# Keeping the intermediate activations in HBM as bf16, through casting transfers on GpSimd's queue

## The reference

```python
x = x + _layernorm(_L0_attn_ref(_layernorm(x), mask, weight, bias))
x = x + _layernorm(_L0_ffn_ref(_layernorm(x), W_up, gate_w, expert_bias, lora_A, lora_B))
# _L0_attn_ref: einsum('bsk,nk->bsn', data, masked weight) + bias
# _L0_ffn_ref:  x @ W_up.T + delta,  delta = one_hot(argmax(x @ gate_w.T)) picks B_e (A_e x)
```

## Time and profile before

| | us |
|---|---|
| median of 2 runs | 1734.52 (1693.67 and 1775.36) |
| profiled execution | 1690.93 |
| its span, slowest core (core 4) | 1689.4 |
| spans of the 8 cores | 1678.3 to 1689.4 |
| PE busy | 1115.7 (66%) |
| DVE, ACT, POOL busy | 571.7, 404.1, 82.5 |
| closing stage, last matmul to end | about 90 |

### The profile page before, as it was taken

How to read it: one execution, slowest core, us unless ns; L and a number is a source line. 1 busy time by engine, 2 the same in 40 slices (tenths; PEclk the granted TensorE clock), 3 DMA queues, 4 the chain that set the end, 5 groups by cost and what they waited for, 6 DMA issues and landing times.

```text
span 1689.4 us, 26743 instructions; the slowest of 8 cores (1678.3 to 1689.4 us)
## 1 busy us (share of the span) xinstructions
PE 1115.7 (66%) x9240; PEld 869.9 (51%) x9240; DVE 571.7 (34%) x861; ACT 404.1 (24%) x1185; POOL 82.5 (5%) x96
## 2 busy tenths in 40 slices
PE   0122219898988989889321221599999999999800
PEld 0011107676777767667210110377777777777600
DVE  1355445455555555552534334100000000000580
ACT  1224412222222222212323323222222222222200
POOL 1000000000000000000000000000000000000151
PEclk9999999999999999999655555699999999999955
DMA  8820224777667776762333383222442442442299
GB/s 192 289 100 1 50 87 133 184 175 196 163 166 199 171 200 161 174 154 69 119 131 134 117 197 123 78 51 51 76 76 51 76 76 51 76 76 51 79 330 339
DMA packets 40000, 220.47 MB, mean 131 GB/s; under 512 B 4850, under 2 KB 4866, under 8 KB 21442
## 3 DMA queue, kind: packets, MB, share of 16 engines
q0 software_dynamic: 11792, 84.46, 25.5%
q1 hardware_dynamic: 23330, 100.74, 17.9%
q10 hardware_dynamic: 4752, 33.56, 5.3%
HBM read 252.86 MB, written 33.55 MB: 170 GB/s over the span
## 4 chain that ended last, share of the span: by engine, by line
PE 48%; DMA 19%; DVE 16%; issue 8%; ACT 6%; DVEq 1%; ACTq 0%; POOLq 0%; SPq 0%; POOL 0%
PE pm L382 39%; DMA mring<-mw 14%; DVE psj_i L310 4%; PE pt L219 4%; DVE wmb L353 3%; DVE sums_h L263 2%; ACT xbst L278 2%; PE pm L219 2%; ACT mo L547 2%; PE pm L396 2%; ACT junk L533 2%; DMA fm<-xmid 1%; DMA mo<-x 1%; DMA y<-wmb 1%; DVE cmp L573 1%
## 5 line engine op out<-in xcount | busy, mean ns | idle before, releaser
L382 PE MATMUL pm<-wmb,fm 128*128 128x256 bf16 x8192 | 953.9, 275 | 38.8 <-DVE zfm L597 0.7
L382 PEld LDWEIGHTS pm<-wmb,fm 128*128 128x128 bf16 x8192 | 791.9, 99 | 178.4 <-issue 80.7
L402 ACT ACTIVATE mo<-pm 128x256 bf16<-128x256 f32 x256 | 98.3, 384 | 816.1 <-PE pm L389 437.2
L310 DVE TENSOR_REDUCE psj_i<-mring 128x32 int32<-128x1024 int32 x128 | 156.2, 1220 | 222.2 <-DMA mring<-mw 215.8
L219 PE MATMUL pt<-identb,xbst 128*128 128x128 bf16 x264 | 47.2, 289 | 184.9 <-ACT xbst L278 175.4
L188 DVE TENSOR_REDUCE st_d<-acc_s 128x1 f32<-128x16 f32 x8 | 1.4, 170 | 490.8 <-ACT junk L410 490.1
L353 DVE TENSOR_TENSOR wmb<-wmb,bmpj 128x4096 bf16<-128x4096 bf16 x32 | 141.6, 4425 | 11.4 <-DMA wmb<-bw 8.3
L219 PEld LDWEIGHTS pt<-identb,xbst 128*128 128x128 bf16 x264 | 22.7, 115 | 209.3 <-issue 209.2
L410 ACT ACTIVATE junk<-pm 128x256 bf16<-128x256 f32 x256 | 98.3, 384 | 23.8 <-ACT mo L402 0.4
L219 PE MATMUL pm<-identb,mo 128*128 128x128 bf16 x152 | 27.3, 289 | 51.4 <-ACT mo L547 46.1
L225 DVE COPY fm<-pt 128x512 bf16<-128x512 bf16 x72 | 30.6, 424 | 81.5 <-PE pt L219 81.1
(11 more groups left out here) (129 smaller groups left out, 495.9 us busy)
## 6 DMA issues: line engine op xcount, KB each, us to landing
mring<-mw SPq DMA_DIRECT2D x128, 512.0 KB, 5.3
wmb<-bw POOLq DMA_DIRECT2D x32, 1024.0 KB, 10.1
wmb<-bu POOLq DMA_DIRECT2D x32, 1024.0 KB, 7.8
mo<-x POOLq DMA_DIRECT2D x12, 1024.0 KB, 26.4
xst<-x SPq DMA_DIRECT2D x10, 1024.0 KB, 6.9
xmid<-xst ACTq DMA_DIRECT2D x10, 1024.0 KB, 3.9
fm<-xmid SPq DMA_DIRECT2D x8, 1024.0 KB, 11.6
y<-fm ACTq DMA_DIRECT2D x8, 1024.0 KB, 15.8
```

The lines of the kernel that those rows point to most:

```text
L310: return e.tensor_reduce(out=psj_i32[:, (j % 2) * 256 + pc * 32:(j % 2) * 256 + (pc + 1) * 32], in_=mring[idx % 2][:, :].rearrange("p (g w ...
L382: return e.matmul(bank[0:128, 0:NS], fm[:, k * 1024 + i * 128:k * 1024 + i * 128 + 128], wmb[j % 2][:, k * NS:(k + 1) * NS], start=(k == 0 ...
L402: return e.activation(out=mo[:, i * 4096 + j * NS:i * 4096 + (j + 1) * NS], in_=bank[0:128, 0:NS], func=AF.Identity, accum_out=acc_s[:, i ...
```

## The change

`xmid` becomes a bf16 tensor. A transfer between f32 and bf16 has to be issued by POOL, so the store of the middle moves from ACT's queue to POOL's, and the load of the closing stage from SP's queue to POOL's. The f32 slots in SBUF stay as they are. Both get semaphores of the `dP` group, which the first stage used: stores dP4 to dP7, loads dP0 to dP3, each taken again after two chunks. Nothing else is moved: in POOL's stream the 16 stores now stand before the casting loads of the second product (L626 on), and the loads of chunk i+1 in the closing stage stand behind POOL's own addition (L671, half 1) of chunk i.

```diff
-    d_xmid = nc.dram_tensor("xmid", [T, D], F32, kind="Internal").ap()
+    d_xmid = nc.dram_tensor("xmid", [T, D], BF16, kind="Internal").ap()
...
-                xm_tok[(i, h)] = E("scalar", lambda e, i=i, h=h, ap_slot=slots[h][0]: e.dma_start(
+                xm_tok[(i, h)] = E("gpsimd", lambda e, i=i, h=h, ap_slot=slots[h][0]: e.dma_start(
                     out=d_xmid[i * 128:(i + 1) * 128, h * HALF:(h + 1) * HALF], in_=ap_slot),
-                    waits=[trh[h]], inc=store_sem(), amt=16)
+                    waits=[trh[h]], inc="dP%d" % (4 + (2 * i + h) % 4), amt=16)
...
-                semn = slots[h][1] or p6_sems[(2 * i + h) % 4]
                 def fdx(e, i=i, h=h, ap_slot=ap_slot):
                     return e.dma_start(out=ap_slot,
                                       in_=d_xmid[i * 128:(i + 1) * 128, h * HALF:(h + 1) * HALF])
-                td[h] = E("sync", fdx, waits=xw[h] + [xm_tok[(i, h)]],
-                          inc=semn, amt=16)
+                td[h] = E("gpsimd", fdx, waits=xw[h] + [xm_tok[(i, h)]],
+                          inc="dP%d" % ((2 * i + h) % 4), amt=16)
```

## The result

| | before | changed |
|---|---|---|
| median, us | 1693.67 (21 runs) | 1698.68 (22 runs) |
| profiled execution, span of the slowest core | 1689.4 (core 4) | 1692.3 (core 1) |
| middle, first residual add to first matmul of the second product, cores 1 and 4 | 256.1, 256.0 | 250.8, 250.9 |
| closing stage, last matmul to end of the span, mean of 8 cores | 93.2 (89.4 to 96.2) | 102.4 (100.6 to 103.9) |

The ratio is 1.0032, 95% interval [1.0022, 1.0041]: 5 us slower, well inside 2%. The median in the table ahead, 1734.52, was that of two runs of which one, 1775.36, lies 5% above the other, as executions do in which one die of the chip shows a lower clock; twenty-one runs give 1693.67, and all ratios here leave such runs out.

The account below looks back on a forecast made before the run. It took the middle as bound by a chain of small steps on DVE, ACT and TensorE, the end by transfers. 1690.93 - 5.0 + 0 + 12.6 = 1698.5, given as 1699 us; own range 1690 to 1712, full range 1678 to 1742.

Parts of the forecast that it names:

- likeliest case: Whole kernel: the forecast itself, contended pairs in the closing stage, 1690 to 1712 us, chance 0.45.
- part 3: Closing stage: loads in POOL's order form a serial chain of issue, landing, addition; +12.6 us.
- Part 1: Middle: stores leave ACT, so its second square starts earlier, 0.64 us per chunk, 8 chunks; -5.0 us.
- cover of 9.5 us: Middle: a POOL store of `xmid` may take up to 9.5 us at no cost.
- Part 2: Start of second product: `W_up` casts queued behind 16 stores on POOL still land in time, 8 us slack; cost 0.
- contended pair: Closing stage, chunks 4 to 7: two loads sharing the engines with two stores, landing in 12.9 us.
- A: Closing stage: HBM is the limit, so pairs land as if alone, 8.0 us; 1679 us, -0.7%, chance 0.14.
- B: Closing stage: widening casts take twice 2.7 us, adding 32 us; 1731 us, +2.4%, chance 0.20 including anything lengthening the chain 26 us.
- C: Closing stage: a load costs engines 1.35 us, a pair lands in 5.3; about 1662 us, -1.7%, chance 0.06.
- D: Closing stage: still bound by the same 28 MB, stores fill the serial gaps; 1686 us, chance 0.15.

Follow-up runs that it names:

- Experiment 1: Kernel before with only the stores of `xmid` moved from ACT's queue to POOL's, `xmid` still f32, loads still on SP: 0.9982 of before.
- experiment 3: Changed kernel with `xmid` back at f32, same queues and order: 1.0061 of before, closing stage 109.7 us.
- experiment 6: Changed kernel with the closing stage's second-half addition moved from POOL to DVE: 1676.31 us, 0.9874 of before, closing stage 81.1 us.
- experiment 9: Kernel before with only the closing stage's second-half addition moved from POOL to DVE: 0.9988 of before, closing stage 88.3 us.
- experiments 7 and 8: 7: changed kernel with `xmid` loaded as plain bf16 by SP, widened by the addition, 0.9929 of before; 8: the same with all additions on DVE, 0.9851.

## Why the prediction came out as it did

**The time.** 1699 us was predicted and 1698.68 measured, inside the range and inside the likeliest case. Its direction depends on the base. The sum was made against the profiled execution, 1690.93, and said 0.5% more; measured is 0.3% more. Read against the median of two runs, 1734.52, the same number says 2% less, which did not happen. The step that failed there is the footing: the text named the gap between its base and that median but did not forecast which level the runs would keep, and widened the range up to 1742 for it. Beside that a step of the sum failed, in part 3 below.

**Part 1, the middle:** -5.0 predicted, -5.3 measured on the cores (256.1 to 250.8), 0.66 us a chunk instead of 0.64. The casting stores landed after 4.5 us at the median and 5.2 at most, not 7.8: the row taken for them moves twice the bytes. Their cover of 9.5 us held.

**Part 2, `W_up` behind the stores:** 0 predicted, 0 measured. The first of the two joint casts went out at 1060.19 and landed at 1069.26, and TensorE started at 1074.63 without a wait: 5.4 us of slack, where the sum had 8 (the cast before it took 9.9 us, not 8.2). Experiment 1 shows how near that was: SP's two loads of chunk 0 beside it cost 2.9 us.

The rule of the Trainium skill that was weighed there (SBUF — State Buffer, SBUF: two separate sides) shows in one of the 16 loads: POOL's issue at 1591.7 took 1.10 us instead of 0.53 while DVE normalised in bf16 (1591.38, 1.35 us), and ended 0.1 us after it. As said, it moved no term.

**Part 3, the closing stage:** +12.6 predicted; +9.2 as the mean of the cores, +11.3 from the core shown before to the core shown after. As a chain the steps were 13.2, 13.1 and four of 17.4 us; measured 12.2 and 14.0, then 15.4, 22.0, 17.8 and 14.4. The sums agree, 95.9 and 95.7 us. So do the landings on average: from its first issue a contended pair landed after 10.5, 17.0, 12.8 and 10.1 us, 12.6 in the mean, where the sum had 12.9. The reason given does not agree. The sentence that failed is "Halved bytes of `xmid` buy nothing in this sum, since the SBUF side of the load is still f32". They gave 7.3 us (experiment 3 against the changed kernel), and the move of the loads into POOL's order cost 109.7 - 93.2 = 16.5 us with f32, not 12.6. The price of a contended pair, 12.9 us, was made from 324 GB/s of the stage before, in which the stores of `y` and the loads keep each other busy to the end. In the serial order with f32 pairs landed after 13.8 us in the mean and the four contended steps took 20.2, 22.8, 16.4 and 15.2 us in experiment 3, 74.5 together, where the sum had 69.6; bf16 brought them down to 69.5. Two errors of opposite sign, 3.9 us too little for the order and 7.3 us left out for the bytes, nearly cancelled. That the time came out within a microsecond is luck.

**The rivals.** A was right in its premise: fewer bytes of HBM shorten the stage, by 7 us in two pairs of kernels that differ in one line. It was wrong in its mechanism, pairs that land in 8.0 us as if alone (12.6 in the mean), and as an outcome. The Trainium skill's figure of about 358 GB/s of HBM bandwidth a core (DMA: Bandwidth & Descriptors, Where 436 GB/s comes from) pointed that way. The trace agrees in direction, 324 GB/s with f32 from HBM and 343 on the SBUF side with bf16, but not in size: the estimate by that figure was 17 us less, and the runs show 7, with the engines still 0.95 busy. B is refuted: the queue shares show 2.9 us of engine time for a transfer of `xmid` with a cast and without. C is refuted by the same shares, and by pairs that landed after 7.3 and 8.2 us on an idle queue, not 5.3. D, that stores fill the gaps, is refuted by the busy share of 0.82.

**What was overlooked.** The first store of `y` waits for all statistics, and POOL's additions lengthen these: one 0.16 us operation of DVE takes 3.84 us while POOL adds (the row of experiment 6). The prediction took 1617.47 for the first addition from the row and did not ask what set it. It did not matter to the sum, but it is worth 5 us of the closing stage with f32 (experiment 9) and 16 with plain bf16 loads (experiments 7 and 8).

## What to carry to other kernels

When a transfer moves to another engine's queue, write out that queue's order: a load that stands behind an addition which waits for the load before it makes a chain, and here that cost 18 us while the halved bytes gave 7. Where only a cast forces the move, load the narrow type plainly and let the addition widen it: then both sides of the transfer are halved and the queue stays free. Here that paid in full only once POOL's additions were gone (closing stage 88.6, then 72.7 us). A stage whose DMA engines are busy 0.96 of the time can still get shorter by fewer bytes on the HBM side, so price the bytes of both sides separately.

## What was not expected of the hardware

- In the closing stage, halving the HBM side of 12 loads of 1 MB gave 7.3 and 6.8 us (0.6 us a load), though the engine time per transfer, taken over whole executions, did not change with the cast (2.9 us). Halving the SBUF side too, by plain loads from SP's queue, gave another 8.4 us (0.7 a load).
- Small statistics operations of DVE, 0.16 us alone, took up to 3.84 us on the core shown while POOL ran its additions of 4.05 us. With no additions on POOL the first addition of DVE came 11 us after the last matmul on every core, instead of 19 to 27.
- DVE adds 128 x 2048 elements in 2.29 us, whether the first input (the slot) is f32 or bf16; POOL takes 4.05 in either case.
